# A graph layer's epilogue: x reloaded behind three pieces, the output bias added by PE, Pool's pair sums released by DVE's totals

## The chip, the cores and the metric

The kernel runs on one core of one Trainium2 chip. The metric is the device time of an execution in microseconds. Each time given is the median of several executions; the profile is of one execution of its own.

## The reference

The layer is one step of message passing over 6,250 nodes (padded to 6,272) of 128 features and 200,000 edges, sorted by one end. Cut to what matters:

```
h   = relu(layernorm(x))                                   # [6250, 128]
xn  = h @ W_in
W   = (ssp(edge_attr @ W_f1 + b_f1) @ W_f2 + b_f2) * edge_weight
msg = xn[dst] * W                                          # one row per edge
agg = segment_sum(msg, src, 6250)
out = x + ssp(agg @ W_o1 + b_o1) @ W_o2 + b_o2             # ssp(z) = softplus(z) - ln 2
```

All inputs and outputs are fp32. The change lies in the last line alone.

## The kernel before, in words

**Prologue** (to about 90 us): x is loaded into `xs`, normalised, multiplied with W_in and stored as three bf16 parts. `bias_rows` (L855 to L868) makes two rows: `bf2_row` and `bo2_row`, each a bias with the ln 2 of the softplus folded in. It then splits `bf2_row` into three bf16 parts, `bf2_parts`, copied for the 4 tiles of a PSUM bank. In `filter_product` (L1281) PE puts that bias into PSUM with one bf16 matmul against `ones_bf`, ahead of the fp32 products that accumulate on it.

**Main loop** (to about 2312 us): 391 chunks of 512 edges. Of these, 283 are summed within the chunk and then added to four accumulators in HBM, `acc[0]` to `acc[3]`, by Pool's indirect DMAs ("scatters", L597, four per chunk, to the accumulators in turn). The other 108 chunks are sorted into bins and summed by PE into `accT` in SBUF. The whole loop is unrolled in one branch of an `If` on a flag (`both`, L436); the other branch holds a general version, which this input doesn't use. After the branch each engine jumps to the code of the epilogue.

At the end of the branch SP waits for the last node sum (`s_dense`, L534), issues the reload of all of x into `xs` (`reload_nodes`, L500: one DMA of 3136 KB; `xs` shares its space with `binned`, so it can't go before) and waits for all scatters (`after_scatters`, L329).

**Epilogue**: the nodes are taken in 13 pieces (`quad(q)`, NQ = 13) of 4 columns of 128 nodes, the last of 1 column. For each piece:

- SP loads it from the four accumulators, 4 DMAs of 256 KB (L567), into one of 4 slots of `acc_sb`. From piece 4 on it waits for `s_add` of the piece that had the slot.
- Pool adds accumulator 3 to 2 (the pair sum, L647, `s_pair`), when the loads are there.
- DVE adds accumulator 1 to 0 (L1140), and then both halves into `total` (L1145, `s_add`).
- PE transposes `total` (L1402). DVE adds PE's own sums `accT` (L1152, PSUM with SBUF). PE multiplies with W_o1 (L1410, PSUM).
- ACT makes |z + b|, exp and ln (L811, L813, L815). DVE completes the softplus (L1160, PSUM with SBUF) into `hid_o`. PE multiplies with W_o2 (L1417).
- DVE adds `xs` from SBUF to the product in PSUM (L1167, `finish`, `s_o`), and Pool issues the store (L651, 256 KB).

The work is staggered by an order written out by hand. DVE's round q is

```
add_up(q); with_pe_part(q - 1); out_hidden(q - 2); finish(q - 3)
```

that is L1140 and L1145 for piece q, L1152 for q-1, L1160 for q-2 and L1167 for q-3. PE's round q is the transposes of q, W_o1 of q-1 and W_o2 of q-2. Pool's round q is the pair sum of q, then a wait for `finish(q - 4)` and that piece's store. All waits between engines are on semaphores.

Ahead of its rounds DVE adds `bo2_row` to all of `xs` in one operation of 6272 columns (L1133), when the reload has landed.

Of the kernel before, what the change touches and what calls it, by code (L numbers as in the profile page):

```python
# [7 lines left out]
P = 128  # L8
# [10 lines left out]
FW = P + 1  # L19
ACCS = 4  # L20


def gnn_kernel(nc, x, src, src_cols, dst, dst_cols, attr_cols, cutoff_cols, W_in, W_f1, b_f1, W_f2, b_f2, W_o1, b_o1, W_o2, b_o2, out):
# [3 lines left out]
    N, F = x.shape  # L27
# [5 lines left out]
    NB = N // P  # L33
# [20 lines left out]
    with ctx:  # L54
# [225 lines left out]
        s_ost = [sem("out_stored_even"), sem("out_stored_odd")]  # L280
        s_res = sem("residual_ready")

# [161 lines left out]
        def _(sp):  # L444
# [63 lines left out]
            for q in range(NQ):  # L508
                store_parts(q)

            def hybrid_loads():
                def step(k):
                    n, slot = k + 2, (k + 2) % 4
                    if exists(n) and n >= 2:
                        after(sp, s_hp, n - 4)
                        sp.sem_inc(s_sp_go, 1)
                        load_attr(n, slot)
                        after(sp, s_oh, n - 4)
                        sp.sem_inc(s_sp_go, 1)
                        load_dst(n, slot)  # L520
                        if pool_chunk(n):
                            wait(sp, s_same, pool_until(n - 4))
                            sp.sem_inc(s_sp_go, 1)
                            load_src(n, slot)
                    n, slot = k + 1, (k + 1) % 4
                    if exists(n):
                        base = sp.value_load(base_row[0:1, bass.ds(n, 1)], min_val=0, max_val=N - W)
                        after(sp, s_xgp, n - 4)
                        sp.sem_inc(s_sp_go, 1)
                        if n == 0:  # L530
                            after_parts(sp)
                        sp.dma_start(xwin[0:KW, slot, :], xw_parts[bass.ds(base, W), :, :].rearrange("w k f -> k w f")).then_inc(s_xwin[slot], 16)
                hybrid_steps(step)
                sp.wait_ge(s_dense, sums_until(NPE + SLOTS - 2, 1))  # L534
                reload_nodes()
                after_scatters(sp, pool_until(NCH))

            def general_loads():
# [14 lines left out]
                sp.wait_ge(s_xg, NCH)  # L553
                reload_nodes()
                for a in range(ACCS):
                    sp.wait_ge(s_scat[a], 16 * NCH * len(range(a, T, ACCS)))

            sp.wait_ge(s_base, 1)
            both(sp, lambda: sp.value_load(in_order[0:1, 0:1], min_val=0, max_val=1), hybrid_loads, general_loads)


            for q in range(NQ):
                b = quad(q)
                if q >= 4:
                    sp.wait_ge(s_add, q - 3)
                for a in range(ACCS):
                    sp.dma_start(acc_sb[:, q % 4, a, 0:len(b) * F].rearrange("p (b f) -> p b f", f=F),  # L567
                                 acc[a][0:N, :].rearrange("(p b) f -> p b f", b=NB)[:, b[0]:b[-1] + 1, :]).then_inc(s_ald[q % 4], 16)

        @block.gpsimd  # L570
        def _(pool):
# [71 lines left out]
            for q in range(NQ + 4):  # L643
                if q < NQ:
                    n, h = len(quad(q)) * F, q % 4
                    pool.wait_ge(s_ald[h], 16 * ACCS * (q // 4 + 1))
                    nc.gpsimd.tensor_tensor(acc_sb[:, h, ACCS - 2, 0:n], acc_sb[:, h, ACCS - 2, 0:n], acc_sb[:, h, ACCS - 1, 0:n], ALU.add).then_inc(s_pair, 1)  # L647
                if q >= 4:
# [169 lines left out]
        def _(dve):  # L818
# [35 lines left out]

            def bias_rows():  # L855

                dve.wait_ge(s_bias, 1)
                V.tensor_tensor(bo2_row[:, :], ps[7][:, 2 * F:3 * F], bo2_row[:, :], ALU.add)
                link(V.tensor_tensor(bf2_row[:, :], ps[7][:, F:2 * F], bf2_row[:, :], ALU.add))
                link(V.tensor_copy(bf2_hi[:, :], bf2_row[:, :]))  # L860
                link(V.tensor_tensor(bf2_rest[:, :], bf2_row[:, :], bf2_hi[:, :], ALU.subtract))
                link(V.tensor_copy(bf2_mid[:, :], bf2_rest[:, :]))
# [3 lines left out]
                for t in range(T):  # L866
                    last = V.scalar_tensor_tensor(bf2_parts[:, t, :], bf2_rest[:, :], is_row[:, 2:3], bf2_sum[:, :], ALU.mult, ALU.add)
                last.then_inc(s_biasr, 1)  # L868

# [261 lines left out]

            dve.wait_ge(s_last, 16)
            V.tensor_tensor(xs[:, :, :], xs[:, :, :], bo2_row[:, :].unsqueeze(1).to_broadcast([P, NB, F]), ALU.add).then_inc(s_res, 1)  # L1133
            dve.wait_ge(s_res, 1)

# [26 lines left out]
            def finish(q):  # L1162
                b, h = quad(q), q % 2
                dve.wait_ge(s_o2, q + 1)
                if q >= 2:
                    dve.wait_ge(s_ost[h], 16 * stores_until(q - 1, h, 2))
# [14 lines left out]
        def _(pe):  # L1181
# [213 lines left out]
            for q in range(NQ + 2):  # L1395
# [15 lines left out]
                if q >= 2:  # L1411
                    k, h = q - 2, q % 2
                    pe.wait_ge(s_o1s, k + 1)
                    if k >= 2:
                        pe.wait_ge(s_o, k - 1)
                    for j in range(len(quad(k))):
                        ins = MM(ps[6 + h][:, j * F:(j + 1) * F], hid_o[:, h, j * P:(j + 1) * P], w_o2[:, :], start=True, stop=True)  # L1417
                    ins.then_inc(s_o2, 1)
# [50 lines left out]
```

## Time and profile before

| | |
|---|---|
| median of 3 runs | 2403.86 us (2403.68 to 2404.15) |
| the profiled execution | 2405.56 us, span 2403.7 us |
| granted TensorE clock, mean | 0.976 |
| PE busy | 2216.1 us, 92% of the span |
| DVE busy | 1867.4 us, 78% |
| ACT busy | 1786.7 us, 74% |
| POOL busy | 1847.7 us, 77% |
| epilogue, from Pool's last scatter to the end | 2310.97 to 2403.7 us |

The busy shares are means over the whole span; the epilogue is the last 4% of it and has its own limits. In a timeline each row is one instruction, or several of one kind merged ("x8"), with the start in us from the span's start and the duration in us. "[1.99 <-DMA ...]" is the time that the engine had been idle before it, and what released it. In the windows "PEclk" is the clock granted to TensorE as a share of 2.4 GHz, and "DMA" the mean busy share of the 16 DMA engines.

### The profile page before, as it was taken

Reading aid. Unit: us, or ns where it says so; the run is one execution under the profiler, and the core shown is the slowest. Engines: PE = TensorE matmul, PEld = TensorE weight load, DVE = VectorE, ACT = ScalarE, POOL = GpSimd, SP = SyncE. Lnnn points to the kernel's source line nnn. Section 1 sums busy time; section 2 is a strip of 40 time slices with the busy share of each in tenths; the row PEclk is TensorE's granted clock in tenths of the full one; section 3 lists DMA queues with packets and bytes.
Section 4 is the critical chain, followed back from the end, with each engine's and each line's share of the span. In section 5 each row is a group of like instructions: output and inputs, shape, how many; then the busy total and the mean of one; then the engine's idle time right before and its main releaser. Section 6 shows DMA issues by size and latency. Waiting matters only on the chain.

```text
span 2403.7 us, 56748 instructions
## 1 busy us (share of the span) xinstructions
PE 2216.1 (92%) x16758; PEld 1415.3 (59%) x16953; DVE 1867.4 (78%) x3897; ACT 1786.7 (74%) x4171; POOL 1847.7 (77%) x1182
## 2 busy tenths in 40 slices
PE   6699999999999999999999999999999999999945
PEld 4466666666666666666666666666666666666623
DVE  5777777887778777877778877787788778788758
ACT  4587777777777777777777777777777777777703
POOL 1488888788878878888887888878887888888853
PEclk9699999999999999999999999999999999999968
DMA  9466655555565555555556555655555556655564
GB/s 349 129 96 88 90 89 86 88 91 89 86 88 89 88 88 90 88 87 91 86 88 90 87 89 88 89 87 89 88 90 86 87 89 88 88 89 88 76 171 171
DMA packets 350176, 239.86 MB, mean 100 GB/s; under 512 B 89295, under 2 KB 337551, under 8 KB 349539
## 3 DMA queue, kind: packets, MB, share of 16 engines
q0 software_dynamic: 164000, 77.47, 33.6%
q1 hardware_dynamic: 184651, 158.26, 24.7%
q8 instruction: 141, 2.31, 0.4%
q14 instruction: 172, 1.41, 0.2%
q10 hardware_dynamic: 1212, 0.42, 0.1%
HBM read 139.86 MB, written 96.12 MB: 98 GB/s over the span
## 4 chain that ended last, share of the span: by engine, by line
PE 68%; DMA 12%; issue 7%; POOL 6%; ACT 4%; DVE 3%; SPq 0%; ACTq 0%; POOLq 0%; DVEq 0%
PE ps L1304 19%; PE ps L1323 15%; PE ps L1283 12%; DMA acc<-region,target 10%; PE ps L1273 8%; PE ps L1290 8%; POOL acc L597 6%; PE ps L1355 4%; ACT region L740 2%; PE ps L1281 1%; DMA w_f<-in_L_gnn_W_f_dram 1%; ACT region L764 1%; PE ps L1240 0%; DVE region L1152 0%; POOL parts L590 0%
## 5 line engine op out<-in xcount | busy, mean ns | idle before, releaser
L597 POOL DMA_INDIRECT acc<-region,target x1132 | 1800.7, 1591 | 422.0 <-issue 279.3
L1304 PE MATMUL ps<-region 128*128 128x386 bf16 x3024 | 650.7, 336 | 66.4 <-ACT region L740 65.0
L740 ACT ACTIVATE region<-ps 128x386 bf16<-128x386 f32 x756 | 372.3, 492 | 272.4 <-PE ps L1304 265.4
L1323 PE MATMUL ps<-region 64*128 64x448 bf16 x4536 | 497.7, 352 | 9.3 <-DVE region L1035 9.3
L1304 PEld LDWEIGHTS ps<-region 128*128 128x128 bf16 x3024 | 253.9, 97 | 367.2 <-issue 138.3
L996 DVE SCALAR_TENSOR_TENSOR region<-ps,bf_negative,region 128x512 f32<-128x512 f32 x391 | 292.3, 748 | 212.0 <-ACT region L726 211.4
L764 ACT ACTIVATE region<-ps,cut_col 128x128 f32<-128x128 f32 x1564 | 438.9, 362 | 0.6 <-PE ps L1355 0.6
L1283 PE MATMUL ps<-w_f,region 128*128 128x128 f32 x3128 | 416.0, 276 | 11.4 <-issue 0.4
L1283 PEld LDWEIGHTS ps<-w_f,region 128*128 128x128 f32 x3128 | 415.4, 193 | 11.2
L722 ACT ACTIVATE region<-ps,bf 128x512 f32<-128x512 f32 x391 | 269.0, 688 | 71.3 <-PE ps L1273 15.3
L1290 PEld LDWEIGHTS ps<-region 128*128 128x128 f32 x2264 | 294.6, 191 | 24.9 <-DVE region L996 3.2
L1323 PEld LDWEIGHTS ps<-region 64*128 64x128 bf16 x4536 | 191.2, 94 | 196.8 <-issue 14.7
L1290 PE MATMUL ps<-region 128*128 128x129 f32 x2264 | 302.7, 275 | 1.4 <-DVE region L996 0.4
L1050 DVE TENSOR_SCALAR region<-counting,region 128x448 bf16<-128x448 f16 x756 | 289.5, 423 | 8.8 <-PE ps L1323 8.1
L1273 PE MATMUL ps<-attrT,w_f 20*128 20x256 f32 x1564 | 275.6, 428 | 19.0 <-DVE region L996 8.7
L724 ACT ACTIVATE region<-region 128x512 f32<-128x512 f32 x391 | 246.7, 631 | 12.4
L726 ACT ACTIVATE region<-region 128x512 f32<-128x512 f32 x391 | 246.2, 630 | 12.3
L1088 DVE TENSOR_TENSOR region<-ps,region 128x512 f32<-128x512 f32 x283 | 194.9, 689 | 71.9 <-ACT region L764 60.1
L987 DVE TENSOR_SCALAR moved<-region,weight_limit,spare_row 128x4 f32<-128x4 f32 x283 | 107.4, 380 | 130.2 <-ACT region L731 130.2
L1035 DVE TENSOR_TENSOR region<-region,ps 128x896 f32<-128x896 f32 x188 | 202.3, 1076 | 4.3 <-PE ps L1323 4.3
L1273 PEld LDWEIGHTS ps<-attrT,w_f 20*128 20x128 f32 x1564 | 118.2, 184 | 147.0 <-issue 146.9
L980 DVE TENSOR_TENSOR region<-src_b,src_col 128x512 f32<-128x512 int16 x283 | 195.5, 691 | 0.0
(133 smaller groups left out, 1633.2 us busy)
## 6 DMA issues: line engine op xcount, KB each, us to landing
dst_b<-dst_rows SPq DMA_DIRECT2D x391, 128.0 KB
src_b<-src_rows SPq DMA_DIRECT2D x283, 128.0 KB
acc<-region,target POOLq DMA_INDIRECT x1132
attrT<-in_edge_attr_dram SPq DMA_DIRECT2D x782, 20.0 KB
acc<-region SPq DMA_DIRECT2D x20, 640.0 KB, 18.7
xwin<-xw_parts SPq DMA_DIRECT2D x391, 31.5 KB
region<-acc SPq DMA_DIRECT2D x48, 256.0 KB, 4.8
xw_parts<-parts SPq DMA_DIRECT2D x12, 384.0 KB, 2.3
```

The source lines that it names most:

```text
L597: nc.gpsimd.indirect_dma_start(out=acc[a], out_offset=bass.IndirectOffsetOnAxis(ap=target[:, slot, t:t + 1], axis=0), in_=summed[:, slot, ...
L722: nc.scalar.activation(a, z, ACT.Abs, bias=bias).then_inc(steps[0], 1)
L724: nc.scalar.activation(a, a, ACT.Exp, scale=-1.0).then_inc(steps[1], 1)
L740: nc.scalar.activation(binned[:, h, j, :], binned_ps[:, 0:PC], ACT.Copy).then_inc(s_binned, 1)
L764: last = nc.scalar.activation(xg[:, n % 2, t * F:(t + 1) * F], ps[3][:, t * F:(t + 1) * F], ACT.Copy, scale=cut_col[:, bass.ds(n, 1), t])
L996: V.scalar_tensor_tensor(halves(hidden[:, odd, :]), hidden_ps, bf1_negative[:, 0:1], halves(hidden_exp[:, odd, :]), ALU.max, ALU.add).then ...
L1050: V.tensor_scalar(in_node[:, sums_until(kk, i) % 2, slot, :], counting[:, 0:NL], binned[:, slot, j, 3 * F:3 * F + 1], binned[:, slot, j, 3 ...
L1273: ins = MM(hidden_ps[:, r, :], w_f1[rows, :], attrT[rows, slot, :], start=True, stop=True)
L1283: ins = MM(ps[2][:, t * F:(t + 1) * F], hidden[:, odd, t * P:(t + 1) * P], w_f2[:, :], start=False, stop=(t == T - 1), skip_group_check=True)
L1290: ins = MM(sums_ps[t], same[:, odd, t * P:(t + 1) * P], message[:, odd, t, :], start=True, stop=True)
L1304: ins = MM(binned_ps[:, 0:PC], place[:, h % 2, t, j * P:(j + 1) * P], payload_high[:, h % 2, t, :], start=(t == 0), stop=(t == T - 1))
L1323: ins = MM(ps[6 + r][:, 0:NL], binned[rows, slot, j, part * F:(part + 1) * F], in_node[rows, sums_until(kk, i) % 2, slot, :], start=(d == ...
```

## The change

Three things change in the epilogue.

1. **x.** SP no longer reloads x between its two last waits. After both waits, and still inside the branch, it issues the loads of pieces 0, 1 and 2 (`load_first`, EARLY = 3) and the reload of x behind them. The loop behind the branch begins with piece 3. DVE waits for x in `finish(0)`.
2. **The output bias.** L1133 is removed. In its place DVE splits `bo2_row` into three bf16 parts in `bf2_parts`, when the main loop is over. PE puts the bias into the PSUM bank with one bf16 matmul per piece, and the W_o2 products accumulate on it.
3. **Pool's pair sums.** From piece 1 on the pair sum of piece q also waits for `s_add` of q, which is DVE's total (L1145) of piece q-1.

```diff
--- before.py
+++ after.py
@@ -18,6 +18,7 @@
 SLOTS = 4
 FW = P + 1
 ACCS = 4
+EARLY = 3
 
 
 def gnn_kernel(nc, x, src, src_cols, dst, dst_cols, attr_cols, cutoff_cols, W_in, W_f1, b_f1, W_f2, b_f2, W_o1, b_o1, W_o2, b_o2, out):
@@ -278,7 +279,7 @@
         s_o2 = sem("out_in_psum")
         s_o = sem("out_ready")
         s_ost = [sem("out_stored_even"), sem("out_stored_odd")]
-        s_res = sem("residual_ready")
+        s_bo2 = sem("out_bias_parts_ready")
 
         def quad(q):
             return range(EB * q, min(EB * q + EB, NB))
@@ -507,6 +508,17 @@
                 load_dst(c, c)
             for q in range(NQ):
                 store_parts(q)
+
+            def load_accs(q):
+                b = quad(q)
+                for a in range(ACCS):
+                    sp.dma_start(acc_sb[:, q % 4, a, 0:len(b) * F].rearrange("p (b f) -> p b f", f=F),
+                                 acc[a][0:N, :].rearrange("(p b) f -> p b f", b=NB)[:, b[0]:b[-1] + 1, :]).then_inc(s_ald[q % 4], 16)
+
+            def load_first():
+                for q in range(EARLY):
+                    load_accs(q)
+                reload_nodes()
 
             def hybrid_loads():
                 def step(k):
@@ -532,8 +544,8 @@
                         sp.dma_start(xwin[0:KW, slot, :], xw_parts[bass.ds(base, W), :, :].rearrange("w k f -> k w f")).then_inc(s_xwin[slot], 16)
                 hybrid_steps(step)
                 sp.wait_ge(s_dense, sums_until(NPE + SLOTS - 2, 1))
-                reload_nodes()
                 after_scatters(sp, pool_until(NCH))
+                load_first()
 
             def general_loads():
                 def step(i, m):
@@ -551,21 +563,18 @@
                         sp.dma_start(dst_now[:, slot, :], dst_cols[:, bass.ds(c, 1), :].rearrange("p o t -> p (o t)")).then_inc(s_dnow[slot], 16)
                 general_steps(sp, step)
                 sp.wait_ge(s_xg, NCH)
-                reload_nodes()
                 for a in range(ACCS):
                     sp.wait_ge(s_scat[a], 16 * NCH * len(range(a, T, ACCS)))
+                load_first()
 
             sp.wait_ge(s_base, 1)
             both(sp, lambda: sp.value_load(in_order[0:1, 0:1], min_val=0, max_val=1), hybrid_loads, general_loads)
 
 
-            for q in range(NQ):
-                b = quad(q)
+            for q in range(EARLY, NQ):
                 if q >= 4:
                     sp.wait_ge(s_add, q - 3)
-                for a in range(ACCS):
-                    sp.dma_start(acc_sb[:, q % 4, a, 0:len(b) * F].rearrange("p (b f) -> p b f", f=F),
-                                 acc[a][0:N, :].rearrange("(p b) f -> p b f", b=NB)[:, b[0]:b[-1] + 1, :]).then_inc(s_ald[q % 4], 16)
+                load_accs(q)
 
         @block.gpsimd
         def _(pool):
@@ -644,6 +653,8 @@
                 if q < NQ:
                     n, h = len(quad(q)) * F, q % 4
                     pool.wait_ge(s_ald[h], 16 * ACCS * (q // 4 + 1))
+                    if q >= 1:
+                        pool.wait_ge(s_add, q)
                     nc.gpsimd.tensor_tensor(acc_sb[:, h, ACCS - 2, 0:n], acc_sb[:, h, ACCS - 2, 0:n], acc_sb[:, h, ACCS - 1, 0:n], ALU.add).then_inc(s_pair, 1)
                 if q >= 4:
                     b, h = quad(q - 4), q % 2
@@ -852,20 +863,24 @@
                 V.tensor_scalar(bf1_less_ln2[:, :], ones[:, :], bf1[:, 0:1], -LN2, ALU.mult, ALU.add)
                 V.tensor_scalar(bo1_less_ln2[:, :], ones[:, :], bo1[:, 0:1], -LN2, ALU.mult, ALU.add).then_inc(s_shift, 1)
 
-            def bias_rows():
-
-                dve.wait_ge(s_bias, 1)
-                V.tensor_tensor(bo2_row[:, :], ps[7][:, 2 * F:3 * F], bo2_row[:, :], ALU.add)
-                link(V.tensor_tensor(bf2_row[:, :], ps[7][:, F:2 * F], bf2_row[:, :], ALU.add))
-                link(V.tensor_copy(bf2_hi[:, :], bf2_row[:, :]))
-                link(V.tensor_tensor(bf2_rest[:, :], bf2_row[:, :], bf2_hi[:, :], ALU.subtract))
+            def split(row):
+
+                link(V.tensor_copy(bf2_hi[:, :], row[:, :]))
+                link(V.tensor_tensor(bf2_rest[:, :], row[:, :], bf2_hi[:, :], ALU.subtract))
                 link(V.tensor_copy(bf2_mid[:, :], bf2_rest[:, :]))
                 V.tensor_scalar(bf2_sum[:, :], bf2_hi[:, :], is_row[:, 0:1], None, ALU.mult)
                 link(V.tensor_tensor(bf2_rest[:, :], bf2_rest[:, :], bf2_mid[:, :], ALU.subtract))
                 link(V.scalar_tensor_tensor(bf2_sum[:, :], bf2_mid[:, :], is_row[:, 1:2], bf2_sum[:, :], ALU.mult, ALU.add))
                 for t in range(T):
                     last = V.scalar_tensor_tensor(bf2_parts[:, t, :], bf2_rest[:, :], is_row[:, 2:3], bf2_sum[:, :], ALU.mult, ALU.add)
-                last.then_inc(s_biasr, 1)
+                return last
+
+            def bias_rows():
+
+                dve.wait_ge(s_bias, 1)
+                V.tensor_tensor(bo2_row[:, :], ps[7][:, 2 * F:3 * F], bo2_row[:, :], ALU.add)
+                link(V.tensor_tensor(bf2_row[:, :], ps[7][:, F:2 * F], bf2_row[:, :], ALU.add))
+                split(bf2_row).then_inc(s_biasr, 1)
 
             def variances():
                 dve.wait_ge(s_vps, NQ)
@@ -1129,9 +1144,7 @@
             combine(0)
             both(dve, lambda: dve.value_load(in_order[0:1, 0:1], min_val=0, max_val=1), hybrid_work, general_work)
 
-            dve.wait_ge(s_last, 16)
-            V.tensor_tensor(xs[:, :, :], xs[:, :, :], bo2_row[:, :].unsqueeze(1).to_broadcast([P, NB, F]), ALU.add).then_inc(s_res, 1)
-            dve.wait_ge(s_res, 1)
+            split(bo2_row).then_inc(s_bo2, 1)
 
             def add_up(q):
                 n, h = len(quad(q)) * F, q % 4
@@ -1162,6 +1175,8 @@
             def finish(q):
                 b, h = quad(q), q % 2
                 dve.wait_ge(s_o2, q + 1)
+                if q == 0:
+                    dve.wait_ge(s_last, 16)
                 if q >= 2:
                     dve.wait_ge(s_ost[h], 16 * stores_until(q - 1, h, 2))
                 V.tensor_tensor(out_sb[:, h, 0:len(b), :], ps[6 + h][:, 0:len(b) * F].rearrange("p (b f) -> p b f", f=F),
@@ -1413,8 +1428,13 @@
                     pe.wait_ge(s_o1s, k + 1)
                     if k >= 2:
                         pe.wait_ge(s_o, k - 1)
-                    for j in range(len(quad(k))):
-                        ins = MM(ps[6 + h][:, j * F:(j + 1) * F], hid_o[:, h, j * P:(j + 1) * P], w_o2[:, :], start=True, stop=True)
+                    if k == 0:
+                        pe.wait_ge(s_bo2, 1)
+                    n = len(quad(k))
+                    MM(ps[6 + h][:, 0:n * F], ones_bf[:, :], bf2_parts[:, 0:n, :].rearrange("p t f -> p (t f)"), start=True, stop=False, skip_group_check=True)
+                    for j in range(n):
+                        ins = MM(ps[6 + h][:, j * F:(j + 1) * F], hid_o[:, h, j * P:(j + 1) * P], w_o2[:, :],
+                                 start=False, stop=(j == n - 1), skip_group_check=True)
                     ins.then_inc(s_o2, 1)
```

## Rows read from the trace of the kernel before

**Rows 1.** Chain that ended last, 2262 to 2336: start us, us, what.

```profile
2299.85 3.65 DMA acc<-region,target
...
2310.97 12.38 DMA acc<-region,target
...
2323.48 2.72 issue
2326.20 0.33 SPq L567
```

**Rows 2.** Waits of line 329 (scatters): duration ns min/median/max, first and last start.

```profile
L329 SPq EVENT_SEMAPHORE  x2: 17/22/28, 2313.5 to 2323.4; - x2
```

**Rows 3.** Timeline of DVE, epilogue: start us, us, operation [idle before <-releaser].

```profile
2323.20 6.69 DVE L1133 TENSOR_TENSOR region<-region,bo_row 128x6272 f32<-128x6272 f32 x1 [10.52 <-DMA region<-in_x_dram]
2331.89 1.79 DVE L1140 TENSOR_TENSOR region<-region 128x512 f32<-128x512 f32 x1 [1.99 <-DMA region<-acc]
...
2337.27 0.69 DVE L1145 TENSOR_TENSOR region<-region 128x512 f32<-128x512 f32 x1 [1.22 <-POOL region L647]
...
2340.50 1.05 DVE L1152 TENSOR_TENSOR region<-ps,region 128x512 f32<-128x512 f32 x1
2343.15 0.75 DVE L1160 SCALAR_TENSOR_TENSOR region<-ps,bo_negative,region 128x512 f32<-128x512 f32 x1 [1.59 <-ACT region L815]
...
2348.14 0.69 DVE L1140 TENSOR_TENSOR region<-region 128x512 f32<-128x512 f32 x1
...
2358.14 0.68 DVE L1140 TENSOR_TENSOR region<-region 128x512 f32<-128x512 f32 x1
2358.85 2.07 DVE L1145 TENSOR_TENSOR region<-region 128x512 f32<-128x512 f32 x1
2360.84 1.05 DVE L1152 TENSOR_TENSOR region<-ps,region 128x512 f32<-128x512 f32 x1
2361.81 0.74 DVE L1160 SCALAR_TENSOR_TENSOR region<-ps,bo_negative,region 128x512 f32<-128x512 f32 x1
...
2363.07 0.68 DVE L1140 TENSOR_TENSOR region<-region 128x512 f32<-128x512 f32 x1
...
2387.02 0.28 DVE L1140 TENSOR_TENSOR region<-region 128x128 f32<-128x128 f32 x1
```

**Rows 4.** Timeline of POOL, epilogue, same columns.

```profile
2335.40 1.77 POOL L647 TENSOR_TENSOR region<-region 128x512 f32<-128x512 f32 x1 [2.27 <-DMA region<-acc]
...
2340.75 1.28 POOL L647 TENSOR_TENSOR region<-region 128x512 f32<-128x512 f32 x1 [1.44 <-DMA region<-acc]
...
2359.09 1.27 POOL L647 TENSOR_TENSOR region<-region 128x512 f32<-128x512 f32 x1
```

**Rows 5.** Windows: length, busy by engine, PEclk, DMA share, GB/s.

```profile
2314.00:2321.00 7.00, 0.00 (x0) 0.00 (x0) 0.00 (x0) 0.00 (x0) 0.00 (x0) 0.50 1.00 407
...
2348.00:2351.00 3.00, 1.04 (x9) 0.85 (x7) 2.97 (x4) 1.95 (x3) 1.90 (x2) 1.00 0.98 366
...
2337.90:2344.10 6.20, 5.82 (x13) 2.70 (x13) 4.57 (x7) 2.33 (x4) 3.19 (x3) 0.50 1.06 394
```

**Rows 6.** Waits of SP's queue, 2275 to 2404: total us, times, longest.

```profile
SPq L500 <- PE ps L1323: 45.5, 1, 45.5
```

**Rows 7.** Lines of DVE by shape, 62.6 to 66.1: busy us, mean ns.

```profile
L867 DVE SCALAR_TENSOR_TENSOR bf_parts<-bf_rest,is_row,bf_sum 128x128 bf16<-128x128 f32 x4 | 1.1, 348 | 0.0
```

**Rows 8.** Timeline of PE, from 2275: columns as rows 3.

```profile
2278.78 0.38 PE L1281 MATMUL ps<-bf_parts,ones_bf 128*128 128x512 bf16 x1
...
2338.99 2.08 PE L1410 MATMUL ps<-region,w_o 128*128 128x512 f32 x2
...
2356.05 0.66 PE L1402 MATMUL ps<-ident,region 128*128 128x128 f32 x4 [0.77 <-DVE region L1145]
2357.01 1.12 PE L1410 MATMUL ps<-region,w_o 128*128 128x512 f32 x2 [0.31 <-DVE region L1152]
2357.98 1.05 PE L1417 MATMUL ps<-w_o,region 128*128 128x128 f32 x8
```

## Prediction

> **What bounds the kernel now.** I read the page first: the change leaves everything before the epilogue alone, so the only stretch that matters is the last 93 us, from the last scatter to the end of the span. The chain of waits says what sets its start [rows 1]. Three things follow each other there with nothing beside them: the last scatter, 12.38 us from Pool's issue to its landing at 2323.35, where the scatter issued at 2299.85 took 3.65; 2.72 us of "issue" on SP's queue between the end of its wait and its first load of a piece; and the load itself, first issue 2326.20, piece 0 there at 2331.87. SP's waits on the scatters end at 2313.5 and at 2323.4 [rows 2]: the first is for the last but one, issued one slot of 1.86 before 2310.97, so 4.4 us on its way, and only the very last is held.
>
> Then the timeline of DVE, by rounds [rows 3]. A piece's sums, transpose, output layers and store are spread over four rounds, and piece q enters with L1140. Rounds 0 to 3 fill (2331.89 to 2348.14, 16.25 us), rounds 4 to 11 take 2348.14 to 2387.02, 38.9 us or 4.86 each, and from there the drain ends at 2403.7, 16.7 us. In a full round DVE has no gap; its steps, start to start, are L1140 0.71, L1145 1.99, L1152 0.97, L1160 with L1167 1.26: 4.93. The odd one is L1145: 2.07 long there and 0.69 at 2337.27, for the same shape [rows 3]. Pool's timeline gives the reason [rows 4]: its pair sum starts at 2359.09, 0.24 after L1145 at 2358.85, and L1145 ends 0.56 after the pair sum does. DVE waits for Pool. The reverse also happens: the pair sum at 2335.40, begun just behind an L1140, took 1.77 in place of 1.27. So DVE bounds the rounds, and 1.38 us of each is this collision.
>
> **The change part by part.** The sum is made against the profiled execution, span 2403.7 (its own time 2405.56); the median of the runs, 2403.86, is 0.2 above that span, so what I save on the span I take off the median.
>
> *The x reload behind three pieces, start.* It moves 3.21 MB in 2314 to 2321 at 407 GB/s, with the 16 DMA engines fully busy [rows 5], exactly while the last scatter is out. Issued later it cannot hold that scatter. I take the 4.4 of its neighbour: scatters done at 2315.4 in place of 2323.35, 7.9 less. Bounds: 3.65 (8.7 less), and 12.38 unchanged (rival 1). SP's wait for the last node sums, which stays ahead, ended before 2311.6, so it isn't the next thing late.
>
> *The first loads inside the branch.* The 2.72 us lie behind the jump out of the branch, when SP has nothing to wait for. The 12 loads of pieces 0 to 2 and the x load are now ahead of that jump, in line with code that SP has sat in front of for 45.5 us at L500 [rows 6]: 2.7 less (bounds 0 and 2.8; with 0 the result is 2392.7). The jump comes after the x issue, while 6 MB are queued, and is hidden. Together the first piece lands at 2321.1 (2315.4 + 0.1 + 5.67): a shift of 10.7.
>
> *The x reload, where it goes.* Pieces land 2.7 us apart when the queue is full (2335.40 to 2340.75 are two) [rows 4]. x now stands in front of piece 3: 3.21 MB at 407 GB/s is 7.9 us (8.2 at 391). With T the landing of piece 0, pieces 1 and 2 come at T+3.5 and T+6.2 as before, x at T+14, piece 3 at T+16.7. Before, round 3 started at T+12 and ended at T+16.3. Now its L1140 starts with piece 3, together with Pool's pair sum, so it collides as at 2335.40 (L1145 done 2.6 after the landing), and L1152, L1160, L1167 follow in 2.3: end of round 3 at T+21.5. That is 5.2 later (bounds 4.5 and 6).
>
> *The residual add L1133*, 6.69 us, goes away, but it lay under the loads of piece 0 [rows 3]; worth nothing by itself. With it, x need not be there until round 3's L1167. `split(bo2_row)` is added: eight small operations and the four of L867, 0.35 each [rows 7], some 3 us, in DVE's idle time from 2312.7 to 2321.1. If scatters landed at once it would still fit.
>
> *The pair sum released by the total of the piece before.* Pair q now starts when L1145 of q-1 has ended, beside L1152 and L1160 (1.63 us start to start together, 1.27 needed). Both read one operand from PSUM. Pool's pair sum at 2340.75 lay inside L1152 at 2340.50, and neither was longer (1.28, 1.05) [rows 3, 4]; L1160 I take to behave like it, being of the same kind. So L1145 takes 0.61 start to start in place of 1.99, and a round 3.55. What is queued behind Pool's new wait is one store per round, whose input (L1167) comes later than the pair sum anyway. Eight rounds: 28.4 in place of 38.9, 10.5 less.
>
> Does something else end later in a 3.55 us round? *PE*: transposes 0.66, w_o1 1.12, w_o2 1.05 at full clock [rows 8]; the bias matmul is new, 0.38 long at 2278.78, of which the next matmul covers some 0.15, as w_o2 at 2357.98 does of w_o1: 0.22. Together 3.05 of 3.55, and from L1145's end to the end of w_o2 it fits with 0.2 to spare. *ACT's chain*: from L1152's end through w_o1 and three activations to L1160. At half clock w_o1 takes 2.08 from 2338.99 and L1160 starts at 2343.15 [rows 3, 8], so the activations are 2.08 and the chain 4.2; at full clock 3.3, against 3.47 available (a round less L1152's own end). *DMA*: 1.31 MB per round at the 366 GB/s of a full queue with a store in it [rows 5] is 3.58, level with DVE; but the pieces run ahead by 1 to 3 us when the rounds begin. No cost (upper bound 0.4 in each of 6 rounds).
>
> *The clock.* PE idles about 5 us while x loads, and the granted clock is 0.50 (1.2 GHz) after such a pause; in the fill before it stayed at 0.50 through 6.2 us of nearly continuous work, 5.82 busy [rows 5]. So rounds 4 and 5 run at half clock, 5.7 us of PE work each (3.05 by 2.08/1.12). Walking them through in PE's order, L1160 is 0.6 late in round 4 and L1152 and L1160 another 1.4 in round 5: 2.0 in all (bounds 0, and 2 x 2.15). From then on PE is over 85% busy; before, each second round had a 2 us hole and a spell at half clock.
>
> *Drain*: the same latency chain, with the bias matmul under the wait for a store: 0.1 more.
>
> Sum: -7.9 - 2.8 + 5.2 - 10.5 + 2.0 + 0.1 = -13.9, span 2389.8, median 2390.0. Own range with all bounds 2385.5 to 2395.
>
> **Rivals.** 1. *The last scatter takes 12 us anyway*, for being last and not for x. For: it is on another queue than x (Pool's), and after 2310.97 nothing else is like it. Against: its neighbour took 4.4, and it landed 0.15 us after x did (DVE, idle for x, starts at 2323.20 [rows 3]). Then -13.9 + 7.9: 2397.9. The Trainium skill, "DMA: Bandwidth & Descriptors", section "Queues, rings and completion order", bears on both sides: engines take turns between queues by packet, by which x would hold the scatter only for a share of its time; but a completion mark lands after all earlier writes of that DMA engine, across queues, by which the scatter would be seen only with x. The time of landing agrees with the second.
>
> 2. *The collision only moves*: the pair sum stops L1152 or L1160 for 1.4 us, and a round stays 4.9. For: L1152 and L1160 also read SBUF, and I have only overlaps in which they started first. Against: those overlaps cost neither side anything, while L1140's did. Then -13.9 + 10.5 - 2.0 (no cold loss in a longer round): 2398.5. The Trainium skill, "SBUF — State Buffer", section "Who interferes with whom", says that only a DVE operation with two SBUF inputs contends with Pool's reads; by that this rival falls.
>
> 3. *Slower: PE stays at half clock.* The pause for x is followed by rounds with the bias matmul added; if the clock never rises, PE's 5.7 us per round are beyond DVE's 3.55 and the old 4.86: 8 x 5.7 = 45.6, +6.7 in place of -10.5, and the drain about 2.4 longer (a w_o1 and a W_o2 product at half clock). -10.7 + 5.2 + 6.7 + 2.4 = +3.6: 2407.5. It decides from 5.25 us a round. For: there is a half-clock spell in every second round now. Against: PE was then idle for 2 us in that round, and steady work has always ended it.
>
> 4. *The change doesn't do what it says*: pieces stay late from x on and DMA sets the rounds. Then 8 rounds at 4.0: 2393.6, inside the own range.
>
> **How the numbers follow.** Forecast with its own range 0.79 (rival 4 in it), rival 1 0.08, rival 2 0.06, rival 3 0.03, something unnamed 0.04. A measurement here can tell about 0.2%, 4.8 us: from 2399.1 up is no change. Faster 0.90: the forecast, rival 1 and half of rival 2. Same 0.06: the other half, some of rival 3 and of the unnamed. Slower 0.04: rival 3 with a little more on it, and the rest of the unnamed. The range goes from 2385.5 to rival 1's 2398.0; 0.79 and most of 0.08 lie in it.
>
> **What the profile after would show.** SP's first L567-like issue about 0.1 us after the last scatter, near 2315.5, and the last scatter some 4.4 long; DVE idle about 5 us ahead of round 3, released by a load; pair sums beginning at L1145's end and 1.27 long; L1145 at 0.69 in rounds 4 to 11, rounds of 3.55 from the third on; granted clock 1.00 from about 10 us after piece 3. Wrong it would be by a last scatter of 10 us or more, by L1152 or L1160 at 2 us, or by PE at 0.50 in the rounds.

## The result, and the profile after

The changed kernel takes 2385.8 us (median of 4 executions, 2385.4 to 2387.3), before 2404.0 beside it: ratio 0.9927, interval 0.9914 to 0.9940, 18.2 us or 0.7% faster. The forecast was 2390.0, range 2385.5 to 2398.0. The profiled execution has a span of 2383.9 us.

The stretch before Pool's last scatter differs from execution to execution by more than some of the terms in question: in the eleven profiles of this study the last scatter starts anywhere from 2306.8 to 2312.4. So all kernels are compared from there on. A1 to A4 are the four stretches that make up the epilogue; L1153 is the line that was L1140, L1158 was L1145, L1165 L1152, L1173 L1160, L1182 L1167. The values are differences of the starts in the timelines.

| us | before | again | after | again |
|---|---|---|---|---|
| start of the last scatter | 2310.97 | 2309.04 | 2307.74 | 2308.13 |
| A1: from there to the first L1140 / L1153 | 20.92 | 20.95 | 10.10 | 9.19 |
| A2: rounds 0 to 3 | 16.25 | 15.92 | 20.66 | 21.92 |
| A3: rounds 4 to 11 | 38.88 | 38.39 | 29.23 | 29.25 |
| A4: from round 12 to the end | 16.68 | 16.60 | 16.17 | 16.11 |
| last scatter to the end | 92.73 | 91.86 | 76.16 | 76.47 |

The mean of the last row falls from 92.3 to 76.3, by 16.0 us. Single profiles of one kernel differ in A1 and A2 by up to 1.3.

The chain of waits of the changed kernel, columns as in [rows 1]:

```profile
2307.74 3.25 DMA acc<-region,target
...
2311.04 0.05 issue
2311.08 0.34 SPq L515
...
2311.94 1.15 SPq L515
...
2317.65 0.63 SPq L501
...
2318.38 3.52 issue
2321.90 0.33 SPq L515
```

The last scatter has landed 3.25 us after its issue, where it took 12.38 [rows 1]. The first load of a piece (L515) follows 0.09 us behind; the 2.72 us of issue [rows 1] now stand behind the x load (L501) and the jump (L437), as 3.52, while the queue is full. One load took SP 1.15 us in place of 0.43.

DVE's timeline (against [rows 3]) and Pool's (against [rows 4]):

```profile
2317.84 0.69 DVE L1153 TENSOR_TENSOR region<-region 128x512 f32<-128x512 f32 x1 [2.44 <-DMA region<-acc]
...
2328.76 0.75 DVE L1173 SCALAR_TENSOR_TENSOR region<-ps,bo_negative,region 128x512 f32<-128x512 f32 x1 [1.53 <-ACT region L826]
2333.76 0.69 DVE L1153 TENSOR_TENSOR region<-region 128x512 f32<-128x512 f32 x1 [4.25 <-DMA region<-acc]
2335.66 0.69 DVE L1158 TENSOR_TENSOR region<-region 128x512 f32<-128x512 f32 x1 [1.21 <-POOL region L658]
...
2338.50 0.68 DVE L1153 TENSOR_TENSOR region<-region 128x512 f32<-128x512 f32 x1
2339.21 0.69 DVE L1158 TENSOR_TENSOR region<-region 128x512 f32<-128x512 f32 x1
...
2341.53 0.75 DVE L1173 SCALAR_TENSOR_TENSOR region<-ps,bo_negative,region 128x512 f32<-128x512 f32 x1 [0.66 <-ACT region L826]
...
2346.36 0.68 DVE L1153 TENSOR_TENSOR region<-region 128x512 f32<-128x512 f32 x1
2347.07 0.69 DVE L1158 TENSOR_TENSOR region<-region 128x512 f32<-128x512 f32 x1
2347.68 1.06 DVE L1165 TENSOR_TENSOR region<-ps,region 128x512 f32<-128x512 f32 x1
2348.66 0.75 DVE L1173 SCALAR_TENSOR_TENSOR region<-ps,bo_negative,region 128x512 f32<-128x512 f32 x1
2349.32 0.69 DVE L1182 TENSOR_TENSOR region<-ps,region 128x512 f32<-128x512 f32 x1
...
2367.73 0.28 DVE L1153 TENSOR_TENSOR region<-region 128x128 f32<-128x128 f32 x1
```

```profile
2333.81 1.77 POOL L658 TENSOR_TENSOR region<-region 128x512 f32<-128x512 f32 x1 [8.81 <-DMA region<-acc]
...
2346.74 0.56 POOL L662 DMA_DIRECT2D out_dram<-region  x1 [1.11 <-DVE region L1182]
2347.92 1.27 POOL L658 TENSOR_TENSOR region<-region 128x512 f32<-128x512 f32 x1 [0.62 <-DVE region L1158]
...
2377.18 0.54 POOL L662 DMA_DIRECT2D out_dram<-region  x1 [0.96 <-DVE region L1182]
```

Round 3 starts at 2333.76, after 4.25 us in which DVE waits for the loads of piece 3, behind x. There Pool's pair sum and L1153 still collide, as in every round that begins with a landing, because the total that the pair sum waits for is that of the piece before, and was done long ago: L1158 starts 1.90 behind L1153. From round 4 on they don't. The round from 2346.36 to 2349.91 is the regular one: its five steps take 0.71, 0.61, 0.98, 0.66 and 0.59, together 3.55. L1158 is 0.69 long, where L1145 was 2.07 [rows 3], and Pool's pair sum at 2347.92 lies beside L1165 and L1173, which are as long as they were.

PE's timeline (against [rows 8]), and windows of 1 us, whose last three columns are the granted clock, the DMA share and GB/s (against [rows 5]):

```profile
2336.41 1.11 PE L1417 MATMUL ps<-ident,region 128*128 128x128 f32 x4 [5.55 <-DVE region L1158]
2337.38 2.07 PE L1425 MATMUL ps<-region,w_o 128*128 128x512 f32 x2
...
2349.76 0.38 PE L1434 MATMUL ps<-bf_parts,ones_bf 128*128 128x512 bf16 x1
2349.98 1.05 PE L1436 MATMUL ps<-w_o,region 128*128 128x128 f32 x8
```

```profile
2326.00:2327.00 1.00, 1.00 (x4) 0.68 (x4) 1.00 (x2) 0.28 (x1) 0.00 (x0) 0.50 1.02 426
2327.00:2328.00 1.00, 1.00 (x5) 0.43 (x3) 0.23 (x1) 0.97 (x2) 0.00 (x0) 0.91 0.93 401
...
2333.00:2334.00 1.00, 0.00 (x0) 0.00 (x0) 0.24 (x1) 0.00 (x0) 0.19 (x1) 1.00 1.06 391
2334.00:2335.00 1.00, 0.00 (x0) 0.00 (x0) 0.46 (x1) 0.00 (x0) 1.00 (x1) 0.51 1.05 383
...
2340.00:2341.00 1.00, 1.00 (x7) 1.00 (x7) 0.87 (x1) 0.94 (x3) 0.94 (x1) 0.58 1.07 391
2341.00:2342.00 1.00, 1.00 (x9) 0.75 (x7) 0.47 (x1) 0.50 (x1) 0.33 (x1) 1.00 1.06 389
```

The bias matmul (L1434) is 0.38 long, and the W_o2 products start 0.22 behind it. The clock was at 0.50 until 2327, then at 1.00, fell at 2334 after PE had been idle since 2330.85, and rose again at 2340.8 (the 0.58 of the window from 2340 is 0.8 us at half and 0.2 at full clock), 4.4 us after PE had begun to work at 2336.41. From there it stays at 1.00 to the end of the rounds.

### The profile page after: what moved, and what is told of

Read it like the earlier page. It is cut to its first block, busy times and chain, and to the rows that moved or that the text cites. A ratio compares the mean times of both kernels' runs of the same rounds, so it can differ in the third digit from the quotient of the medians.

```text
span 2383.9 us, 56991 instructions
## 1 busy us (share of the span) xinstructions
PE 2222.2 (93%) x16966; PEld 1409.9 (59%) x16966; DVE 1850.6 (78%) x3906; ACT 1788.6 (75%) x4171; POOL 1849.1 (78%) x1182
## 4 chain that ended last, share of the span: by engine, by line
PE 58%; DMA 18%; POOL 8%; issue 8%; ACT 5%; DVE 3%; SPq 0%; ACTq 0%; POOLq 0%; DVEq 0%
DMA acc<-region,target 16%; PE ps L1319 16%; PE ps L1338 13%; PE ps L1298 9%; POOL acc L606 7%; PE ps L1288 7%; PE ps L1305 6%; PE ps L1370 3%; PE ps L1296 2%; ACT region L751 2%; ACT region L775 1%; DMA w_f<-in_L_gnn_W_f_dram 1%; ACT region L733 1%; ACT region L735 1%; DMA region<-acc 0%
```

## Experiments

Each kernel was timed against the kernel before on the same chip. "Last scatter to the end" is from its profile, as in the table.

**Only the pair sums released by the total.** The kernel before with one edit.

```diff
                     pool.wait_ge(s_ald[h], 16 * ACCS * (q // 4 + 1))
+                    if q >= 1:
+                        pool.wait_ge(s_add, q)
```

> The kernel before with one edit alone: from piece 1 on, Pool's pair sum also waits for the total of the piece before. Theory A (the three parts are separate terms, each as the two traces show it): full rounds go from 4.93 to 3.56 us, the last scatter still takes some 12 us and SP's jump 2.7 us: 2404.0 - 10 = 2394, interval 2393 to 2395. Theory B (the rounds are short only because x and the residual add are out of the way, for instance since the pieces run late otherwise): rounds of 4 us or more, 2397 or above. Theory C (the collision moves to L1152 or L1160): 2403 to 2404.

Measured: 2391.1 against 2402.3, ratio 0.9957 (0.9940 to 0.9973), 11.2 us faster. Last scatter to the end 78.63. DVE's timeline in the rounds:

```profile
2340.73 0.68 DVE L1142 TENSOR_TENSOR region<-region 128x512 f32<-128x512 f32 x1
2341.44 0.69 DVE L1147 TENSOR_TENSOR region<-region 128x512 f32<-128x512 f32 x1
2342.05 1.05 DVE L1154 TENSOR_TENSOR region<-ps,region 128x512 f32<-128x512 f32 x1
...
2344.29 0.68 DVE L1142 TENSOR_TENSOR region<-region 128x512 f32<-128x512 f32 x1
```

All rounds from round 3 on are 3.56 to 3.58, and A3 is 28.50. A2 is 14.76, 1.2 to 1.5 shorter than before: 0.8 of that is round 3 (3.56, before 4.32 and 4.42), which the pair sums shorten like the others, and the rest is round 0, whose length goes mainly by when piece 1 lands (2.75 here, 2.6 to 3.8 in the eleven profiles, with and without the new wait). That is theory A: the rounds need nothing of the other two parts. B and C fall. The median lies 2 us under theory A's interval; the kernel before is itself 1.7 faster here than the 2404.0 from which that was worked out, and the last scatter was shorter. It took 10.23 us here, 1.6 to 2.2 less than in the two profiles of before. The chain of waits and SP's timeline show why:

```profile
2307.17 10.23 DMA acc<-region,target
```

```profile
2305.34 0.35 SPq L500 DMA_DIRECT2D region<-in_x_dram  x1
```

In this execution x was issued 1.83 us ahead of the last scatter, in the first profile of before 0.62 us behind the start of it, and the scatter landed at 2317.40, 12.06 after x's issue. In the kernel before that was 11.76 (2311.59 to 2323.35). The scatter's landing follows x, not its own issue.

**All but the pair sums.** The changed kernel without that wait.

```diff
-                    if q >= 1:
-                        pool.wait_ge(s_add, q)
```

> The changed kernel without Pool's new wait: x behind three pieces, loads inside the branch, bias by PE. Theory A: the start of the epilogue gives 10.8 us, x ahead of piece 3 takes 4.4 back, the rounds stay at 4.9: 2404.0 - 6.4 = 2397.6 (2396.5 to 2399). Theory B: there is more behind it than these two, among it what made the main loop of the changed kernel's profile end 3.2 us earlier: 2394 to 2395.

Measured: 2395.7 against 2402.3, ratio 0.9973 (0.9962 to 0.9983), 6.7 us faster; last scatter to the end 85.84, 6.5 less than the mean of before. A1 9.71, A2 21.72, A3 38.26, A4 16.15. Theory A (its interval, worked out from 2404.0, is missed by 0.8), and the last scatter starts at 2311.46: the early start in the profile of the changed kernel doesn't come with this part.

**Only the bias by PE.** The residual add goes, and the reload and all loads stay where they were. The edit is against the changed kernel.

```diff
 in the branch:
                 sp.wait_ge(s_dense, sums_until(NPE + SLOTS - 2, 1))
+                reload_nodes()
                 after_scatters(sp, pool_until(NCH))
-                load_first()
 behind it:
-            for q in range(EARLY, NQ):
+            for q in range(NQ):
...
 Pool: without the wait for s_add
```

> The kernel before with the output bias by PE alone: L1133 gone, x waited for in finish(0), reload and loads where they were, no new wait on Pool. Theory A: L1133 lay under the loads and the bias matmul lies under DVE's rounds: 2404 within 1 us, last scatter 12 us. Theory B (removing 6.7 us of DVE work or the bias matmul's warmer PE is worth something in the fill or the drain): 2401 to 2403. Theory C (PE's extra work delays rounds): 2405 or above.

Measured: 2402.8 against 2402.3, ratio 0.9999 (0.9989 to 1.0009). Last scatter to the end 92.38. Its last scatter, in the chain of waits:

```profile
2309.02 13.36 DMA acc<-region,target
```

So L1133's 6.7 us were worth nothing, as forecast, and the bias matmul costs nothing. In the trace A4 is 16.18, 0.4 to 0.5 below before; the kernels with the bias by PE have 16.1 to 16.2 as well (all but x in four parts), and the one with only the pair sums 16.57. All of it lies behind the issue of the last store, when DVE and PE have finished: from there to the end are 7.12 to 7.22 us in the three profiles with the bias by DVE and 6.65 to 6.75 in the eight with it by PE, and the last store lands 2.2 to 2.4 us after its issue in the former and 1.8 in the latter. Why is open. It is too small to be seen in the medians, and A1, with 13.36 for the scatter, goes the other way.

**The first loads outside the branch.**

```diff
                 after_scatters(sp, pool_until(NCH))
-                load_first()
...
+            load_first()
             for q in range(EARLY, NQ):
```

> The changed kernel with the loads of pieces 0 to 2 and x behind the branch and not in it. Theory A (the 2.72 us on SP's queue were the jump out of the branch): last scatter 3 to 4.5 us as in the changed kernel, then about 2.8 us of issue ahead of the first load: 2385.8 + 2.7 = 2388.5 (2388 to 2389.5). Theory B (they belonged to the state of SP's queue behind the x transfer): no such gap, 2385.8.

Measured: 2387.7 against 2402.7, ratio 0.9940 (0.9923 to 0.9956); last scatter to the end 78.41. The chain:

```profile
2312.39 3.27 DMA acc<-region,target
...
2315.75 0.05 SPq L437
2315.80 2.63 issue
2318.43 0.34 SPq L515
```

The scatter is at 3.27, and behind the jump there are 2.63 us of issue before the first load. Theory A: the gap goes with the jump, whatever the queue has just moved. A1 is 12.79, 2.7 and 3.6 more than in the two profiles of the changed kernel, and 2.1 us of it reach the end (78.41 against 76.3). Only the traces show this: the 15.0 us gained here and the 18.2 and 15.3 of the changed kernel are too near each other for the medians to tell. The Trainium skill, "Runtime: NRT & Kernel Launch", section "Instruction fetch mechanics", says that a taken branch to code outside what is loaded forces a fetch before the engine can go on; the traces agree in that 2.46 to 3.85 us stand behind SP's jump in nine of the eleven profiles, and do not show the fetch apart. In the two kernels below in which 16 loads stand ahead of the jump, x in four parts and x out of the queue, it is only 1.7 and 0.4 us; why is open.

**x ahead of piece 0**, but behind the scatters.

```diff
             def load_first():
+                reload_nodes()
                 for q in range(EARLY):
                     load_accs(q)
-                reload_nodes()
```

> The changed kernel with x issued behind the wait for the scatters as there, but ahead of piece 0. Theory A (x held up the last scatter, and in the queue it costs 8 us before whatever stands behind it): last scatter 3 to 4.5 us; piece 0 lands 7.5 to 8 us later than in the changed kernel, round 3 then waits for nothing, so that 8 - 4.4 = 3.6 remain: 2389.4 (2388.5 to 2390.5). Theory B (the last scatter is slow or fast by chance or by its place): last scatter near 12 us, 2397 or above.

Measured: 2385.0 against 2402.7, ratio 0.9930 (0.9913 to 0.9947). Last scatter to the end 75.85, 0.3 to 0.6 less than the changed kernel. The chain and DVE's rounds 0 and 4:

```profile
2306.75 3.20 DMA acc<-region,target
...
2310.05 0.35 SPq L501
```

```profile
2323.24 0.69 DVE L1153 TENSOR_TENSOR region<-region 128x512 f32<-128x512 f32 x1 [8.81 <-DMA region<-acc]
...
2337.96 0.69 DVE L1153 TENSOR_TENSOR region<-region 128x512 f32<-128x512 f32 x1
```

On the scatter theory A holds: 3.20 us, with x in the queue right behind it, against 10.2 to 13.4 in the four profiles in which x is issued around it. On the size it fails: I expected 3.6 us lost, and nothing is. Piece 0 lands 6.4 later than in the first profile of the changed kernel (A1 16.49; 7.3 later than in the second), not 8, probably since x moves while the loads behind it are being issued. The fill takes 14.72 in place of 20.66, since nothing stands in front of piece 3. Its round 3 is 3.55, 0.8 less than before by the pair sums, which in the changed kernel is lost in the wait for piece 3. And round 4 has no half-clock loss (A3 28.48). Against the first profile that makes 6.39 - 5.94 - 0.75 = -0.3. The place of x, ahead of piece 0 or behind piece 2, doesn't matter within what these runs can tell; that it is behind the last scatter does.

**x in four parts**, behind pieces 3, 6, 8 and 10.

```diff
-EARLY = 3
+EARLY = 4
...
             def reload_nodes():
-                sp.dma_start(xs[:, :, :], ...).then_inc(s_last, 16)
+                load_nodes(0)
...
                 load_accs(q)
+                if q in (6, 8, 10):
+                    load_nodes((q - 4) // 2)
...
-                if q == 0:
-                    dve.wait_ge(s_last, 16)
+                if q in (0, 3, 6, 9):
+                    dve.wait_ge(s_xs[q // 3], 32)
```

> The changed kernel with x reloaded in four parts (12, 12, 12 and 13 columns), behind pieces 3, 6, 8 and 10, each waited for in the round that first needs it (finish of 0, 3, 6 and 9). Theory A (DVE's idle time ahead of round 3 is only x standing in front of piece 3): the 4.2 us idle goes away, a fraction of it comes back where the DMA queue can't keep a round of 3.56 us with x parts in it: 2382 to 2384, idle ahead of round 3 under 1 us. Theory B (the queue is the bound of the whole epilogue, in whichever order): 2385.8 within 0.7, with the idle time spread over rounds 4 to 11.

Measured: 2384.5 against 2402.3, ratio 0.9926 (0.9909 to 0.9943); last scatter to the end 75.13. DVE's timeline, and a window over rounds 8 to 10:

```profile
2329.79 0.68 DVE L1154 TENSOR_TENSOR region<-region 128x512 f32<-128x512 f32 x1
...
2333.35 0.67 DVE L1154 TENSOR_TENSOR region<-region 128x512 f32<-128x512 f32 x1
...
2351.72 0.69 DVE L1154 TENSOR_TENSOR region<-region 128x512 f32<-128x512 f32 x1
2353.63 0.69 DVE L1159 TENSOR_TENSOR region<-region 128x512 f32<-128x512 f32 x1 [1.21 <-POOL region L659]
...
2360.30 0.69 DVE L1154 TENSOR_TENSOR region<-region 128x512 f32<-128x512 f32 x1 [0.20 <-DMA region<-acc]
```

```profile
2350.00:2358.00 8.00, 5.27 (x28) 3.38 (x28) 6.63 (x11) 3.39 (x7) 4.09 (x4) 1.00 1.05 402
```

Both theories have a part, and the median lies just outside both intervals. The idle time ahead of round 3 is gone (A2 15.49), and 2.5 of it comes back in rounds 7 to 11, which take 3.8 to 4.8 (A3 31.70). The two of 4.75, 9 and 11, have an x part ahead of the piece and begin with its landing, so that in them the collision is back: L1159 waits 1.21 for Pool. Another 1.0 comes back in the drain, where PE, after 1.8 us of idle time, had a granted clock of 0.50 from 2364.1 to 2367.5. In rounds 8 to 10 the DMA engines are fully busy at 402 GB/s: 1.31 MB for a round and 3.21 MB of x are what the queue has to move, in whichever order.

**The kernel before once more.**

> The kernel before unchanged, once more with a profile. Theory A (the 3.2 us by which the main loop of the changed kernel's profile ended earlier is scatter between executions): Pool's last scatter starts somewhere between 2306 and 2312 us in this profile, and not at 2310.97 again. Theory B (the change shortened the main loop): it starts within 0.5 us of 2310.97. In both the last scatter takes 12 us, the rounds 4.9 us.

Measured: 2402.7 in one execution, span 2400.9; last scatter to the end 91.86. The last scatter:

```profile
2309.04 11.86 DMA acc<-region,target
```

It starts 1.93 earlier than in the first profile. Theory A.

**x out of the queue.** `parts` is free after the prologue and holds 24 columns of x, and 6 more lie in `xs` behind `binned`. They are reloaded during the main loop; 19 columns are left for the epilogue.

```diff
-EARLY = 3
+EARLY = 4
+X_AT = {200 + 10 * i: i for i in range(8)}
...
+        x_first = parts[:, :, :, :, :].rearrange("p a b k f -> p (a b k f)").bitcast(fp32).rearrange("p (b f) -> p b f", f=F)
...
+            def reload_early(i):
+                if i < 6:
+                    reload_nodes(quad(i), x_first[:, 4 * i:4 * i + 4, :], 0)
+                else:
+                    b = range(43 + 3 * (i - 6), 46 + 3 * (i - 6))
+                    reload_nodes(b, xs[:, b[0]:b[-1] + 1, :], 1)
...
                 def step(k):
+                    if k in X_AT:
+                        reload_early(X_AT[k])
...
                 load_accs(q)
+                if q in (6, 9):
+                    reload_late((q - 6) // 3)
```

> The changed kernel with x out of the epilogue's queue as far as space goes: 24 of its 49 columns are reloaded into the space of parts and 6 in place, by 8 DMAs spread over steps 200 to 270 of the main loop; 12 columns follow piece 6 and 7 follow piece 9; pieces 0 to 3 are issued inside the branch. Theory A (what is left of x in the changed kernel is its place in the queue, 4.4 us ahead of piece 3 or 6 us ahead of piece 0, and the pair sums keep rounds at 3.56 us): last scatter to end 70 to 71.5 us in place of 76.2, median 5 us below the changed kernel, the main loop unchanged. Theory B (the queue is near its limit anyway): rounds of 3.7 to 4 us behind piece 6, 73 to 75 us. Theory C (the early loads hold up the scatters of the main loop as the old reload held the last): main loop 2 us or more longer, nothing gained.

Measured: 2380.2 against 2403.5, ratio 0.9898 (0.9882 to 0.9915). Last scatter to the end 69.68. Rounds 0, 4 and 12 in DVE's timeline:

```profile
2318.34 0.69 DVE L1170 TENSOR_TENSOR region<-region 128x512 f32<-128x512 f32 x1 [1.10 <-DMA region<-acc]
...
2334.16 0.68 DVE L1170 TENSOR_TENSOR region<-region 128x512 f32<-128x512 f32 x1
...
2362.67 0.29 DVE L1170 TENSOR_TENSOR region<-region 128x128 f32<-128x128 f32 x1
```

A1 9.12, A2 15.82, A3 28.51, A4 16.23. Every round from round 3 on is 3.55 to 3.57, and the last scatter starts at 2309.22, within the spread of the others. Theory A, and more than it said: 6.6 us less in the trace than the changed kernel's 76.3, and 8.0 less in the median than the 2388.2 of the changed kernel on the same chip, where I expected 5. This is the fastest kernel of the study.

**The changed kernel once more.**

> The changed kernel unchanged, on the same chip as x_early and with a second profile. Theory A (the 3.2 us by which the main loop of its first profile ended earlier is scatter between executions): median 17 +- 2 us below before, last scatter to end 76 us within 0.5, the last scatter's start anywhere from 2306 to 2312.5. Theory B (it is part of the change): start within 0.5 us of 2307.7.

Measured: 2388.2 against 2403.5, ratio 0.9934 (0.9918 to 0.9951), 15.3 us faster, with the profile in the table above. The last scatter starts at 2308.13, 0.4 from the first profile, which is within what theory B allows. But kernels that differ from it only behind that point start it at 2306.75 (x ahead of piece 0) and 2312.39 (loads outside the branch), so nothing in the change need be behind it. What makes the main loop longer or shorter by up to 5 us is open. Of the two pairs, 18.2 and 15.3, the mean is 16.8, near the 16.0 of the traces.

## Why the prediction was right, step by step

| step | forecast | trace |
|---|---|---|
| the last scatter no longer held by x | -7.9 | -9.1 |
| first loads in line, not behind the jump | -2.8 | -2.8 |
| first load to piece 0 | 0 | +1.1 |
| x in front of piece 3 | +5.2 | +4.4 |
| eight rounds at 3.55 | -10.5 | -10.4 |
| half clock after the pause | +2.0 | +0.7 |
| drain | +0.1 | -0.5 |
| sum | -13.9 | -16.6 |

The trace column is first profile against first profile; its A1 is the first three rows, A2 the fourth, A3 the rounds and the clock. In the second pair of profiles the sum is -15.4. The mechanism was right in all rows but two small ones, the landing of the first load and the drain, which I had at nothing or near it and whose causes are open. The size was partly luck: 2385.8 lies 0.3 us inside the range, and a part of what carried it there is in none of the terms.

*Start.* Both mechanisms are shown by experiments of their own (x ahead of piece 0; loads outside the branch). The scatter was mis-sized: 3.25, below my bound of 3.65; when the neighbour whose 4.4 I took landed, x had been issued for 1.9 us. A slower first landing, 6.74 from the first issue in place of 5.67, gave 1.1 of it back, which I hadn't foreseen; in the second profile it is 5.87, and what sets it is open. Rival 1 is out: with x behind it, the scatter took 3.19 to 3.27 us in each of seven profiles. Of the two rules of the Trainium skill, "DMA: Bandwidth & Descriptors", section "Queues, rings and completion order", that I weighed, the one of completion marks that land behind earlier writes fits these landings, 0.1 to 0.6 us after x's own, and turns by packet alone do not explain them; the runs don't show what happens inside the DMA engines.

*x.* Counted from the first load's issue, round 3 started 22.7 us on, where I had 22.4, after 4.25 us idle where I said 5. The 0.8 is the other side of the late piece 0: what stood behind it in the queue was not late with it. In the second profile piece 0 comes 0.9 earlier and round 3 1.3 later after it, so the term is +6.0 there (A1 and A2 together are 30.8 and 31.1; forecast 31.7). What I did not see is that round 3 itself would get shorter by 0.8 through the pair sums, had it not to wait for piece 3, and so that x costs the same at either place.

*Rounds.* 3.56 against 3.55, with the collision gone and not moved: rival 2 is out, by L1165 and L1173 at their old lengths beside the pair sum. The margins of 0.2 for PE and ACT's chain held, as did the DMA queue, at 285 GB/s from round 4 to round 11, so rival 4 is out too.

*Clock.* The step that failed in its length: I took the 6.2 us at 0.50 of the fill before as what PE needs, and it was 4.4 here (4.2 in the second profile). Only round 4 is late, 4.30 with 0.66 of waiting for ACT, and round 5 is not. Rival 3 is out.

*The rest.* The drain is 0.5 shorter, which bias by PE alone gives too: the last store lands sooner, cause open. `split` has six small operations, not the eight I counted, and with the four of L875 takes 2.9 us, as forecast. The measured 18.2 is 4.3 more than forecast: 2.7 by the terms above, and 1.6 in none of them. The main loops of the two profiles end 3.2 apart, and such differences come between executions of one kernel as well, so the 1.6 is chance as far as is known. The second pair, 15.3, is 1.4 more than forecast.

*Not additive.* The pair sums alone give 11.5 in the trace when the 2.1 by which A1 was shorter there are taken off, the rest alone 6.5, and both 16.0: 2 us less than the sum. Of these, 0.8 is the shorter round 3, which is lost in the wait for x, 0.7 the half-clock round, and 0.5 the shorter round 0 of that one profile, which has nothing to do with the pair sums.

## What to carry to other kernels

When a last small transfer opens the next stage by its landing, hold back the large one that could go now: it costs its time in the queue anyway, and issued around the small one it delays that too (by 7 to 10 us here). Where operations of two engines hold each other up when both read SBUF alone, as Pool's pair sum and DVE's additions do here, release the one beside operations that read PSUM, and look for a store or a wait that happens to place it elsewhere. A release by the other engine's earlier work does not help in a round that begins with a late landing. When a large reload stands in a filled queue, moving it within the queue shifts idle time; only bytes that leave the queue (here 30 of 49 columns, 24 of them into space that had become free) give it back.

## What the runs showed of the hardware

- Pool's scatter of 128 rows landed in 3.2 to 3.3 us (seven profiles) with nothing large issued until it had landed, and in 10.2 to 13.4 us (four profiles) when a load of 3.21 MB was issued on SP's queue between 1.8 us ahead of it and 0.6 us behind. In all four it landed 11.6 to 12.7 us after that load's issue, and 0.1 to 0.6 us after the load itself.
- SP's first instruction behind the jump out of the branch came 2.46 to 2.79 us after it in the five profiles in which it had been waiting, 3.4 to 3.85 us in the four in which it had just issued 12 loads and x, and 1.7 and 0.4 us in the two with 16 loads ahead of the jump. DVE's came 3.05 us after its last operation of the loop in the changed kernel, 3.07 to 3.41 in six other profiles, and 6.71 in the kernel with only the bias by PE, where x was being loaded meanwhile.
- A DVE addition with both inputs in SBUF and Pool's pair sum hold each other up: L1145 took 2.07 to 2.16 us in place of 0.69 when the pair sum began 0.2 to 0.3 us behind it, and the pair sum 1.77 in place of 1.27 when it began 0.05 behind an L1140 or L1153. A DVE operation with one input in PSUM and one in SBUF does not, also when it starts while Pool's is under way (L1173 at 2348.66, in the pair sum from 2347.92 to 2349.19). The Trainium skill, "SBUF — State Buffer", section "Who interferes with whom", says the same of DVE instructions with at most one SBUF input, outside the 2-port performance modes.
